# Fused attention and gated FFN on one core: the first hi half on VectorE, two rows of chunk 0's statistics through memory, a value product moved ahead of the first turns

## The reference

```python
xn = layernorm(x)                                   # 2048 tokens x 512
# attention on xn, with a second layernorm inside it
h  = layernorm(xn) * gamma + beta
q, k, v = h @ Wq, h @ Wk, h @ Wv
out = softmax(causal(q @ k.T / sqrt(512))) @ v @ Wo + xn
# gated FFN, the hidden kept 2 of 4 by magnitude
f  = keep_2_of_4(silu(xn @ Wgate) * (xn @ Wup)) @ Wdown
result = x + out + f
```

## Time and profile before

| | |
|---|---|
| median of 3 runs | 805.35 us (805.06 to 805.59) |
| profiled execution | 806.16 us, of which span 804.3 us |
| TensorE matmul busy | 798.9 us (99%) |
| VectorE busy | 579.5 us (72%) |
| ScalarE busy | 304.9 us (38%) |
| GpSimd busy | 13.8 us (2%) |
| 16 DMA engines | 117.56 MB moved, mean 146 GB/s |

### The profile page before, as it was taken

The page is one execution under the profiler, slowest core; times in us unless marked ns, Lnnn a source line. Parts: engine busy times, 40 slices in busy tenths (PEclk is TensorE's granted clock), DMA queues, the critical chain, the costliest instruction groups (busy, mean ns, idle before and its releaser), DMA issues.

```text
span 804.3 us, 9565 instructions
## 1 busy us (share of the span) xinstructions
PE 798.9 (99%) x3644; PEld 662.6 (82%) x3644; DVE 579.5 (72%) x1004; ACT 304.9 (38%) x500; POOL 13.8 (2%) x33
## 2 busy tenths in 40 slices
PE   9999999999999999999999999999999999999998
PEld 6888888888888888878887888888888888888886
DVE  6978767556632448769989889799559559559786
ACT  5433222123111225554636436265234234335441
POOL 2010101000000000000000000000000000000000
PEclk9999999999999999999999999999999999999999
DMA  9431442040101027466444443496457262261002
GB/s 328 169 132 51 141 138 77 28 144 28 65 27 65 17 100 290 183 249 257 189 166 158 200 167 121 163 360 273 171 206 255 114 227 91 102 233 55 1 0 106
DMA packets 30285, 117.56 MB, mean 146 GB/s; under 512 B 2928, under 2 KB 2976, under 8 KB 27808
## 3 DMA queue, kind: packets, MB, share of 16 engines
q1 hardware_dynamic: 26064, 109.35, 36.5%
q10 hardware_dynamic: 4176, 7.60, 2.8%
HBM read 74.98 MB, written 41.97 MB: 145 GB/s over the span
## 4 chain that ended last, share of the span: by engine, by line
PE 96%; DMA 2%; DVE 1%; ACT 1%; issue 0%; SPq 0%; DVEq 0%; ACTq 0%
PE bank L699 12%; PE bank L701 12%; PE bank L700 11%; PE bank L525 10%; PE bank L527 10%; PE bank L526 10%; PE bank L602 8%; PE bank L773 7%; PE bank L775 7%; PE bank L774 7%; PE bank L586 2%; DMA dw_raw<-L_ffn_w_down 1%; DMA wsum<-w_units 1%; PE bank L649 0%; ACT wset L835 0%
## 5 line engine op out<-in xcount | busy, mean ns | idle before, releaser
L699 PE MATMUL bank<-X_hi,wset 128*128 128x512 f32 x448 | 174.8, 390 | 0.7 <-ACT g_sum L917 0.7
L701 PE MATMUL bank<-X_hi,wset 128*128 128x512 f32 x448 | 174.4, 389 | 0.0
L700 PE MATMUL bank<-X_lo,wset 128*128 128x512 f32 x448 | 174.4, 389 | 0.0
L699 PEld LDWEIGHTS bank<-X_hi,wset 128*128 128x128 f32 x448 | 84.1, 188 | 19.4 <-ACT g_sum L917 1.7
L701 PEld LDWEIGHTS bank<-X_hi,wset 128*128 128x128 f32 x448 | 84.1, 188 | 17.5
L700 PEld LDWEIGHTS bank<-X_lo,wset 128*128 128x128 f32 x448 | 84.1, 188 | 17.3
L773 PE MATMUL bank<-dw,hs_hi 128*128 128x512 f32 x224 | 87.3, 390 | 0.0
L774 PE MATMUL bank<-dw,hs_hi 128*128 128x512 f32 x224 | 87.2, 389 | 0.0
L775 PE MATMUL bank<-dw,hs_lo 128*128 128x512 f32 x224 | 87.2, 389 | 0.0
L1270 DVE TENSOR_TENSOR acc<-bank,acc 128x512 f32<-128x512 f32 x60 | 40.8, 687 | 41.0 <-PE bank L775 40.8
L525 PE MATMUL bank<-xT_hi,zg_hi 128*128 128x512 f32 (+3 forms) x160 | 58.4, 365 | 0.0
(11 more groups left out here) (175 smaller groups left out, 1371.1 us busy)
## 6 DMA issues: line engine op xcount, KB each, us to landing
w_operands<-wset SPq DMA_DIRECT2D x8, 3584.0 KB, 11.8
wset<-w_operands SPq DMA_DIRECT2D x8, 3584.0 KB, 11.4
wsum<-w_units SPq DMA_DIRECT2D x28, 256.0 KB, 3.3
dw_raw<-L_ffn_w_down SPq DMA_DIRECT2D x14, 512.0 KB, 5.0
xw<-L_attn_x SPq DMA_DIRECT2D x4, 1024.0 KB, 9.6
xt_raw<-x_t SPq DMA_DIRECT2D x8, 512.0 KB, 7.3
xn_t<-xt_raw SPq DMA_DIRECT2D x8, 512.0 KB, 5.2
acc<-resid SPq DMA_DIRECT2D x2, 2048.0 KB, 9.3
```

The costliest lines, as they stand in the source:

```text
L699: pe.matmul(dst[:], u[:, 0, :], x_hi, start=(first and kt == 0), stop=False, skip_group_check=True)
L700: pe.matmul(dst[:], u[:, 0, :], x_lo, start=False, stop=False, skip_group_check=True)
L701: last = pe.matmul(dst[:], u[:, 1, :], x_hi, start=False, stop=(kt == 1), skip_group_check=True)
```

## The change

Four edits.

1. The hi half of Wq's piece 0 is cast by VectorE (a `tensor_copy`, semaphore `first_hi_ready`) and no longer by ScalarE. SP issues the loads in the order Wk, Wq for each piece. One `warm` multiplication fewer (8 for 9).
2. `x_rows` and `x_turn` for rows 0 and 1 of chunk 0 are gone, on all three engines. Instead `row_turn` of chunk 1 turns the 32 numbers of chunks 0 and 1 at once, VectorE copies 32 rows for 16, SP stores them together, and behind the load of chunk 1's rows a second load spreads rows 0 and 1 of chunk 0 (`spread0_loaded`, on which `xn[0]` now waits).
3. With that, the waits on `rows_kept` at the first `attend` and at the third turn bank are replaced by a wait for the first eight products.
4. `v[0][2]` moves from between the scores of tile 1 and `attend` of tile 0 to ahead of `head` of tile 0.

```diff
-    steps += [..., xw_load[3], ("x_rows", 0, 1), v[0][0],
-              ("scores", 0, 0), exp[0], ("x_turn", 0, 1), x_scale[1], row_copy[1], v[0][1], row_turn[1], row_store[1], row_spread[1]]
+    steps += [..., xw_load[3], v[0][0],
+              ("scores", 0, 0), exp[0], x_scale[1], row_copy[1], v[0][1], row_turn[1], row_store[1], row_spread[1], v[0][2]]
...
-    beside = {0: [v[0][2]],
-              1: [xh_pre[1][0], v[0][3], xh[1][0]],
+    beside = {1: [xh_pre[1][0], v[0][3], xh[1][0]],
...
-                for m in (0, 1):
+                for m in (1, 0):
                     sp.dma_start(w_raw(m, k), qkv_tiles[m, k]).then_inc(w_loaded[m][k], 16)
...
-                    sp.dma_start(row_stats_dram[n].rearrange("v t p -> (v t) p"), rows_turned_t[0:4 * TC, :]).then_inc(row_stat_stored, 16)
+                    c = 0 if n == 1 else n
+                    sp.dma_start(row_stats_dram[c:n + 1].rearrange("c v t p -> (c v t) p"),
+                                 rows_turned_t[0:(n + 1 - c) * 4 * TC, :]).then_inc(row_stat_stored, 16)
                 elif kind == "row_spread":
...
+                    if n == 1:
+                        sp.dma_start(spread[0][:, 0:2, :], row_stats_dram[0, 0:2].rearrange("v t p -> v (t p)").partition_broadcast(P)
+                                     ).then_inc(spread0_loaded, 16)
...
-                pe.wait_ge(w_hi_ready[left], q + 1)
                 pe.wait_ge(w_hi_ready[right], q + 1)
+                if left == q == 0:
+                    pe.wait_ge(first_hi_ready, 1)
+                else:
+                    pe.wait_ge(w_hi_ready[left], q + 1 if left else q)
...
-            for _ in range(9):
+            for _ in range(8):
                 pe.matmul(o_bank[:], warm[:, 0:P], warm[:], start=True, stop=True)
...
-                        pe.wait_ge(rows_kept, 4)
+                        pe.wait_ge(prod_free, 2 * KT)
...
+                if kind == "split_hi" and (n, k) == (0, 0):
+                    dve.wait_ge(w_loaded[0][0], 16)
+                    nc.vector.tensor_copy(turned[0][0][:, 0, :], w_raw(0, 0)).then_inc(first_hi_ready, 1)
...
                     if n == 0:
-                        dve.wait_ge(rows_kept, 4)
+                        dve.wait_ge(spread0_loaded, 16)
```

More of the change, by code:

```diff
@@ L562, in row_bank_free @@
             def row_bank_free(no):
-                if no < TURN_RING - 1:
+                if no < TURN_RING:
                     pe.wait_ge(prod_free, 2 * KT)
-                elif no == TURN_RING - 1:
-                    pe.wait_ge(rows_kept, 4)
             def turn_rows(n):
+                c = 0 if n == 1 else n
                 no = turn_no["row_turn", n]
@@ L575, in turn_rows @@
                 pe.wait_ge(scale_ready, n + 1)
-                pe.transpose(turn_bank[no % TURN_RING][0:4 * TC, 0:P], row_stat[:, n, :, :, :].rearrange("p v t o -> p (v t o)"),
+                pe.transpose(turn_bank[no % TURN_RING][0:(n + 1 - c) * 4 * TC, 0:P], row_stat[:, c:n + 1, :, :, :].rearrange("p c v t o -> p (c v t o)"),
                              ident[:]).then_inc(turn_full, 1)
@@ L660, in _ @@
                 elif kind == "x_turn":
-                    pe.wait_ge(prod_free, 2 if k == 0 else 2 * KT)
-                    for i, row in ((0, 2), (1, 3)) if k == 0 else ((2, 0), (3, 1)):
+                    pe.wait_ge(prod_free, 2)
+                    for i in range(2):
                         pe.wait_ge(rows_wide_ready, i + 1)
                         for t in range(TC):
-                            last = pe.transpose(row_bank[row][:, t * P:(t + 1) * P], rows_wide[:, row, t, :], ident[:])
+                            last = pe.transpose(bank[i][:, t * P:(t + 1) * P], rows_wide[:, i, t, :], ident[:])
                         last.then_inc(rows_turned, 1)
@@ L859, in _ @@
             for kind, n, k in steps:
-                if kind == "split_hi":
+                if kind == "split_hi" and (n, k) != (0, 0):
                     act.wait_ge(w_loaded[n][k], 16)
@@ L872, in _ @@
                 elif kind == "x_turn":
-                    act.wait_ge(rows_turned, 2 * k + 2)
-                    for row in (2, 3) if k == 0 else (0, 1):
-                        nc.scalar.copy(spread[0][:, row, :], row_bank[row][:]).then_inc(rows_kept, 1)
+                    act.wait_ge(rows_turned, 2)
+                    for i in range(2):
+                        nc.scalar.copy(spread[0][:, 2 + i, :], bank[i][:]).then_inc(rows_kept, 1)
                 elif kind in ("qk_weight", "vo_weight", "z", "v"):
@@ L1112, in _ @@
             for kind, n, k in steps:
-                if kind == "split_lo":
-                    dve.wait_ge(w_hi_ready[n], k + 1)
+                if kind == "split_hi" and (n, k) == (0, 0):
+                    dve.wait_ge(w_loaded[0][0], 16)
+                    nc.vector.tensor_copy(turned[0][0][:, 0, :], w_raw(0, 0)).then_inc(first_hi_ready, 1)
+                elif kind == "split_lo":
+                    if (n, k) == (0, 0):
+                        dve.wait_ge(first_hi_ready, 1)
+                    else:
+                        dve.wait_ge(w_hi_ready[n], k + 1 if n else k)
                     nc.vector.tensor_tensor(turned[n][1][:, k, :], w_raw(n, k), turned[n][0][:, k, :].bitcast(F32),
@@ L1141, in _ @@
                     dve.wait_ge(scale_ready, 1)
-                    for row in (2, 3) if k == 0 else (0, 1):
-                        nc.vector.tensor_scalar(rows_wide[:, row, :, :], row_stat[:, 0, row, :, :].broadcast_to((P, TC, P)), 1.0, None,
+                    for i in range(2):
+                        nc.vector.tensor_scalar(rows_wide[:, i, :, :], row_stat[:, 0, 2 + i, :, :].broadcast_to((P, TC, P)), 1.0, None,
                                                 ALU.mult).then_inc(rows_wide_ready, 1)
@@ L1175, in _ @@
                         dve.wait_ge(row_stat_stored, 16 * (n - 1))
-                    nc.vector.tensor_copy(rows_turned_t[0:4 * TC, :], turn_bank[no % TURN_RING][0:4 * TC, 0:P]).then_inc(turn_free, 1)
+                    lines = (2 if n == 1 else 1) * 4 * TC
+                    nc.vector.tensor_copy(rows_turned_t[0:lines, :], turn_bank[no % TURN_RING][0:lines, 0:P]).then_inc(turn_free, 1)
                 elif kind == "xh":
```

9 lines of the change are left out of this document (4 added, 5 removed).

## The result

In 18 runs of each the changed kernel took 807.17 us (806.15 to 808.04) and the kernel before 805.61 (805.06 to 807.29). The ratio is 1.0016, with a 95% interval of 1.0010 to 1.0022: about 1.3 us slower, 0.8 to 1.8 (the two medians lie 1.56 apart). The forecast was 806.9, or +1.58. The profiled execution took 807.17 us, its span 805.2 (804.3 before, +0.9).

What follows compares the result with a forecast made beforehand. TensorE, busy 798.9 of 804.3 us, was taken to bound the kernel. +0.07 - 0.90 + 0.82 + 0.30 + 1.29 = +1.58 us on the median 805.35 gave 806.9, own range 806.4 to 807.4 (chance 0.70), wider range 804.9 to 808.0.

Steps and rivals of the forecast that it cites:

- the 53 us below which it would have called itself wrong: Tile 1's turns forecast at 53.7 us for 52.11; the prediction is wrong if they come before 53 us.
- start, with piece 3: Kernel start: earlier cast gains at most 0.23 us, swapped loads at piece 3 take it back; +0.07 us.
- transposes: Before the value product near 43.4 us: eight transposes removed, all of it TensorE's time; -0.90 us.
- wait for the statistics: Turn of the statistics near 46 us: TensorE arrives earlier and waits for `scale_ready`; +0.82 us, bounds 0.70 to 0.95.
- wait for `pT_lo`: At `attend` of tile 0: TensorE waits for `pT_lo`, seen at about 51.65 us; +0.30 us.
- wait for the exponential: At tile 1's turns: only `attend` covers maximum and exponential, a chain of 1.84 us; wait +1.29 us.
- has nothing to do with the transposes, so it ends when it did: Chunk 1's statistics chain through GpSimd and VectorE was claimed to end at 46.77 us, unchanged.
- The shift stays to the end: Behind tile 1's turns each stretch between waits keeps its length, so +1.58 us lasts to the program's end.
- its whole list of waits is one entry: TensorE in the kernel before was said to wait only once, 1.2 us at the very start.
- A: Rival at tile 1's turns: the exponential does not wait, only the statistics' wait counts; 805.3 us, chance 0.12.
- B: Rival, full gain: neither statistics nor exponential makes TensorE wait; 804.2 us, faster, chance 0.08.
- C (the clock): Rival: waits or a start gap lower TensorE's clock, eight to fifteen matmuls at 0.43 us; 809 us, chance 0.10.

Runs made afterwards that it cites:

- the changed kernel with the FFN edit: Changed kernel with ScalarE's casts of down weights (n = 4) and weight set (n = 1) behind the two bank snapshots, VectorE's lo halves later: 819.19 us, ratio 1.0162.
- the kernel that swaps piece 0 alone: Before with edits 1 to 3, statistics' turn behind tile 1's scores, only piece 0 loading Wk first: 805.20 us, ratio 0.9993.
- before with either FFN edit: Before with ScalarE's casts at n = 4 and n = 1 behind the snapshots, 817.31 us; or only n = 4's, VectorE's lo halves sooner, 807.00 us.
- The failed FFN edit: ScalarE's casts at n = 4 and n = 1 behind the bank snapshots, VectorE's lo halves later, in four kernels: ratios to before 1.0136, 1.0162, 1.0126, 1.0129.
- the late turn with that edit: Before with edits 2 and 3, statistics' turn behind tile 1's scores, FFN casts behind the snapshots and VectorE's lo halves later: 816.86 us, ratio 1.0129.

## Why the prediction was right, step by step

It was right in sign and mechanism, and right in size for the whole, partly by luck. Two of its terms were too large, by 0.48 and 0.28; two smaller ones made up 0.26 of that. So tile 1's turns come 0.50 ahead of the forecast, only 0.19 behind the 53 us below which it would have called itself wrong. The medians of the runs lie as far apart as forecast, 1.56 for 1.58, though the trace shows only 1.08 at this place. Predicted and measured, in us at tile 1's turns:

| step | predicted | measured |
|---|---|---|
| start, with piece 3 | +0.07 | +0.06 |
| transposes | -0.90 | -0.81 |
| wait for the statistics | +0.82 | +0.34 |
| wait for `pT_lo` | +0.30 | +0.31 |
| wait for the exponential | +1.29 | +1.01 |
| slower first matmuls behind a turn or a wait | not there | +0.17 |
| sum | +1.58 | +1.08 |

*Start.* Right to 0.01, and by the path that was named: the cast's price, and the swapped landing at piece 3 that takes the gain back. ScalarE's second cast ends at 13.85 (13.73 was forecast) and TensorE goes on at 13.90. In part this is luck: the load landed 0.3 us later than forecast and the two casts took 1.14 us for 1.30. In another execution with the same start (the changed kernel with the FFN edit) that load landed 0.8 us later again and the last scores of tile 0 began at 44.13 for 43.33. In the kernel that swaps piece 0 alone there is no gap at piece 3, in one execution whose loads also landed 0.2 us sooner.

*Transposes.* 0.81: the product behind them starts at 43.44 - 0.06 for 44.19. The prediction also counted the slow first matmul behind the transposes (0.32 for 0.23), but one like it (43.44 to 43.73) is there without them.

*Statistics.* The wait is where it was predicted, but 0.34 instead of 0.82. The step that failed is "has nothing to do with the transposes, so it ends when it did". The first of GpSimd's six instructions took 0.60 us in before and takes 0.23 without VectorE's wide copies of edit 2. It is 0.59 to 0.60 in all five kernels with the copies (before, edit 1 alone, edit 4 alone, and before with either FFN edit) and 0.23 in all nine without. In before, the timelines of VectorE and of GpSimd:

```profile
42.41 0.73 DVE L1143 TENSOR_SCALAR rows_wide<-row_stat 128x512 f32<-128x512 f32 x2
```

```profile
42.58 0.60 POOL L513 TENSOR_SCALAR var_eps<-mean_var 128x4 f32<-128x4 f32 x1 [23.27 <-DVE mean_var L1126]
```

GpSimd's instruction begins 0.17 us into the two copies, which end at 43.14, and ends at 43.18, just behind them; the row of after stands above. So removing VectorE's "idle" work was worth 0.3 us on the path after all. The Trainium skill has the rule that I passed over (SBUF — State Buffer, section "SBUF: two separate sides"): VectorE in a two-port mode and GpSimd share one pair of ports, one of them holds it for a whole instruction, and the other is blocked until then. The trace agrees, 0.60 us for 0.23, with one thing to add: the two copies are two instructions, GpSimd's begins during the first and ends only behind the second.

*Exponential.* The chain of 1.84 was exact. The 0.28 too much are 0.13 of latency (TensorE began 0.05 behind ScalarE, not 0.18), 0.09 because the slower first matmul of `attend` covers that much more, and 0.06 because the maximum began 0.11 ahead of `attend` and not 0.05. This wait makes the loss: with edit 4 the stretch is 1.44 us longer than in before and 1.36 longer than without the edit in the changed kernel, and taking the edit out of the changed kernel wins 1.5 us in the runs.

*Behind.* "The shift stays to the end" holds in the attention, which ends 1.14 late. Behind it the FFN's waits for loads add or take up to a microsecond, by how the loads land: the spans differ by 0.9 in the one profiled pair, the runs by 1.3. How the 0.3 between 1.0 and 1.3 arises isn't shown; it is inside the interval. The first reading of the waits, "its whole list of waits is one entry", was wrong by three, and the "no idle time later" that was built on it with it. "To the end" also takes the stretch behind the last matmul for unchanged. For the changed kernel that holds (3.57 us for 3.57), for edits 2 and 3 without edit 1 it is off by 1.1.

*Rivals.* A and B are out: both waits are there. C (the clock) did not come: the spacings behind 7 us are 0.23 between the waits, and 0.29 to 0.33 once directly behind a wait or a turn. The failed FFN edit shows waits that C would have needed: in before with that edit the matmuls stood 0.43 us apart behind 3.85 us of idle time, and behind 2.90 they did in three of the four kernels. The longest wait of after, once the clock is up, is 0.84.

## What to carry to other kernels

Before moving a piece of work ahead of a wait, look at what it covered where it stood: write down when the next consumer's input is ready and how much of the in-order engine's time is left in between. Here 1.39 us of cover were left, and the piece taken out was 2.75 long. And when the bounding engine is 99% busy, the waits in the list that are a few tenths long deserve the whole span's look: they may follow transfers, and then they swallow or add more than the change is worth. Below a microsecond, compare stretches between two instructions of the same trace, not times from the span's start, and include the stretch from the last matmul to the span's end: that is where edits 2 and 3 lost what they had won.

## What the runs showed that was not expected

- A 4-column GpSimd instruction took 0.60 us beside a wide single-source copy of VectorE and 0.23 without it, in 14 traces without an exception (5 and 9).
- The last store of the result landed 3.1 us behind its issue and not 2.0 in exactly the four kernels that have edits 2 and 3 without edit 1, and each of these ends 1.1 us later behind its last matmul. Nothing in those edits touches that store.
- TensorE fell to its lower clock behind 3.85 us of idle time and stayed there for 2.7 us (six matmuls), in before with the FFN edit. In the changed kernel with that edit the six matmuls behind the same wait were fast, and the 0.43 us spacing came behind a second wait of 0.91 us just after them. The other wait of the failed FFN edit, 2.90 us idle in all four kernels, was followed by starts 0.43 us apart in three (in two of them only from the fourth or fifth matmul on, for some 3.4 us) and by 0.23 throughout in the fourth, the late turn with that edit. The waits of 0.15 to 1.1 us that stand by themselves left the clock where it was.
- The instant at which the clock first rises differs between executions of nearly the same start: the last matmul before the spacing shrinks began between 3.7 and 6.3 us. In the four with before's start, the scores of tile 0 differ by 0.7 us.
